# Loading the activation tiles of a banded-attention and MoE layer in pairs of two

## What is computed

```python
x = _layernorm(x + attn(x, w_q, b_q, w_k, b_k, w_v, b_v, w_o, b_o))
x = _layernorm(x + ffn(x, gate_w, gate_b, w1, b1, w2, b2))
# attn: q, k, v = x @ w + b; scores of each token with its 7 neighbours, softmax, @ v, @ w_o + b_o
# ffn:
logits = xf @ gate_w + gate_b
top_w, top_i = top_k(logits, 2)
comb = zeros(n, 8).at[arange(n)[:, None], top_i].add(softmax(top_w))
for ei in range(8):
    h = relu(xf @ w1[ei] + b1[ei])      # w1[ei]: 1024 x 4096
    y = h @ w2[ei] + b2[ei]             # w2[ei]: 4096 x 1024
    out = out + comb[:, ei:ei + 1] * y
```

## Time and profile before

| what | us |
|---|---|
| median of 2 runs | 4987.21 |
| the two runs | 4957.83 and 5016.59 |
| the profiled execution | 4956.09 |
| its span on the slowest core, from first to last instruction | 4953.2 |
| spans of the 8 cores | 4941.5 to 4953.2 |
| start to the first q matmul, half 0 | 77.65 |
| start to the first q matmul, half 1 | 2534.65 |

### The profile page before, as it was taken

How to read it: one execution, slowest core, us unless ns; L and a number is a source line. 1 busy time by engine, 2 the same in 40 slices (tenths; PEclk the granted TensorE clock), 3 DMA queues, 4 the chain that set the end, 5 groups by cost and what they waited for, 6 DMA issues and landing times. The chain is left out here.

```text
span 4953.2 us, 53689 instructions; the slowest of 8 cores (4941.5 to 4953.2 us)
## 1 busy us (share of the span) xinstructions
PE 4303.1 (87%) x19624; PEld 1913.9 (39%) x19624; DVE 1155.8 (23%) x3024; ACT 1091.2 (22%) x2172; POOL 148.7 (3%) x192
## 2 busy tenths in 40 slices
PE   4645589999999999999975554999999999999998
PEld 2222234444444444444432222344444444444443
DVE  0344411122211222111213444022111222112223
ACT  2222222211122111221242222211222111221113
POOL 0000000000000000000000000000000000000000
PEclk9656579999999999999986665899999999999999
DMA  5100034444454444444630000454444544544443
GB/s 86 19 13 9 5 56 80 68 79 75 69 84 69 76 78 68 79 75 72 104 76 17 13 9 6 66 82 69 76 78 68 82 72 71 83 69 77 77 68 85
DMA packets 149771, 310.94 MB, mean 63 GB/s; under 512 B 3641, under 2 KB 4025, under 8 KB 149453
## 3 DMA queue, kind: packets, MB, share of 16 engines
q0 software_dynamic: 144096, 289.49, 36.4%
q1 hardware_dynamic: 5422, 18.03, 1.1%
HBM read 588.60 MB, written 8.39 MB: 121 GB/s over the span
## 5 line engine op out<-in xcount | busy, mean ns | idle before, releaser
L999 PE MATMUL m_pY<-m_w2b,m_hg 128*128 128x512 bf16 x8192 | 1778.8, 379 | 74.1 <-ACT m_hg L976 72.7
L959 PE MATMUL m_pH<-s_xt,m_w1b 128*128 128x512 bf16 x8192 | 1782.2, 380 | 0.0
L1014 DVE SCALAR_TENSOR_TENSOR m_acc<-m_pY,s_comb,m_acc 128x512 f32<-128x512 f32 x1024 | 721.7, 747 | 2955.6 <-PE m_pY L999 2955.6
L976 ACT ACTIVATE m_hg<-m_pH,s_b1pc 128x512 bf16<-128x512 f32 x1024 | 705.9, 689 | 2859.4 <-PE m_pH L959 2859.4
L999 PEld LDWEIGHTS m_pY<-m_w2b,m_hg 128*128 128x128 bf16 x8192 | 796.6, 98 | 1056.3 <-issue 105.4
L959 PEld LDWEIGHTS m_pH<-s_xt,m_w1b 128*128 128x128 bf16 x8192 | 802.4, 98 | 971.8 <-issue 7.9
L510 PE MATMUL h_pj<-h_v_tm,h_attnT 128*128 128x64 bf16 x256 | 54.4, 212 | 261.8 <-DVE h_attnT L503 261.8
L465 ACT ACTIVATE h_a_bf<-h_smx,h_nmx 128x134 bf16<-128x134 f32 x256 | 104.4, 408 | 360.4 <-DVE h_nmx L455 340.7
L510 PEld LDWEIGHTS h_pj<-h_v_tm,h_attnT 128*128 128x128 bf16 x256 | 26.8, 105 | 302.2 <-issue 302.2
L286 PE MATMUL h_pj<-h_xt_ext,s_wbuf 128*128 128x512 bf16 (+1 forms) x640 | 118.7, 344 | 27.2 <-PEq L57 27.2
L447 DVE SCALAR_TENSOR_TENSOR h_smx<-h_pj,s_consts,s_masks 128x134 f32<-128x134 f32 x176 | 61.3, 349 | 295.1 <-PE h_pj L437 294.5
(11 more groups left out here) (95 smaller groups left out, 1213.8 us busy)
## 6 DMA issues: line engine op xcount, KB each, us to landing
m_w1b<-w POOLq DMA_DIRECT2D x64, 2048.0 KB, 16.0
m_w2b<-w POOLq DMA_DIRECT2D x64, 2048.0 KB, 15.9
h_x_own<-xh SPq DMA_DIRECT2D x16, 512.0 KB, 3.4
out<-s_ostg SPq DMA_DIRECT2D x16, 512.0 KB, 2.7
s_xb<-xh POOLq DMA_DIRECT2D x16, 256.0 KB, 3.8
s_wbuf<-wq POOLq DMA_DIRECT2D x2, 2048.0 KB, 25.0
s_wbuf<-wk POOLq DMA_DIRECT2D x2, 2048.0 KB, 36.3
s_wbuf<-wv POOLq DMA_DIRECT2D x2, 2048.0 KB, 15.9
```

Source lines behind the costliest of these rows:

```text
L959: e.matmul(pH[jj % 2][:, 0:512], w1b[0][:, ic * GCOLS + j * 128: ic * GCOLS + j * 128 + 128], xt1[:, ic * HALF_T + ts * 512: ic * HALF_T + ...
L976: e.activation(hg[:, j * HALF_T + ts * 512: j * HALF_T + ts * 512 + 512], pH[jj % 2][:, 0:512], AF.Relu, bias=b1pc[:, e_i * 32 + g_i * 8 + ...
L999: e.matmul(pY[t % 2][fs][:, 0:512], hg[:, j * HALF_T + t * 128: j * HALF_T + t * 128 + 128], w2b[0][:, j * GCOLS + fs * 512: j * GCOLS + f ...
L1014: e.scalar_tensor_tensor(acc[:, t * D + fs * 512: t * D + fs * 512 + 512], pY[t % 2][fs][:, 0:512], comb[:, t * 8 + e_i: t * 8 + e_i + 1], ...
```

## The change

The loads of tiles 2 to 7 of a half are made in pairs. After the transposes of tiles 1, 3 and 5 one DMA, `emit_xld_pair`, brings tiles t + 1 and t + 2, 256 consecutive rows, into both slots of `xb`. It waits for the last transpose of both of the tiles that were there. Both tiles then count on the semaphore `sXB0`. Tile 8 is loaded as before, after the transposes of tile 6. Nothing is issued any more after the transposes of tiles 0, 2 and 4. The rest is unchanged.

```diff
+                def emit_xld_pair(t):
+                    src = xh_d.ap()[B + t * 128: B + t * 128 + 256, :]
+                    src = src.rearrange("(a p) n -> p a n", p=128)
+                    dst = xb[:, 0:2 * D].rearrange("p (a n) -> p a n", a=2)
+                    ev = p.op("pool",
+                              lambda e, src=src, dst=dst:
+                              e.dma_start(dst, src),
+                              waits=[xtr_ev[(t - 2, 7)], xtr_ev[(t - 1, 7)]],
+                              inc="sXB0", k=16)
+                    xld[t] = ev
+                    xld[t + 1] = ev
...
-                    if t + 2 < 9:
-                        emit_xld(t + 2)
+                    if t in (1, 3, 5):
+                        emit_xld_pair(t + 1)
+                    elif t == 6:
+                        emit_xld(8)
```

## The result

The kernel with pairs takes 0.55% longer: the ratio to before is 1.0055, with a 95% interval of 1.0040 to 1.0069. Of 4950 us this is 27 us (20 to 34). Of all executions the medians are 4992.98 us (43 of them, from 4977.99) and 4969.46 us (42, from 4950.13); disturbed executions of several hundred us are among both, and the ratio leaves them out. The profiled execution of the kernel after took 4986.8 us, that of before 4956.1 us.

The account below looks back on a forecast made before the run. TensorE, busy 87% of the span, was taken to bound the kernel, with A1 made of exposed waits. Delays of 14.4 us (half 0) and 14.2 us (half 1), together 28.6 us on 4956.1 us, gave 4985 us; range 4968 to 5045.

Parts of the forecast that it names:

- L: Time in block A1 from a pair's issue to its first tile's first transpose: 5.61 us in half 0, 6.23 in half 1.
- the rounds: Two tiles' turn in A1, costing 6.35 + L us: 12.0 us in half 0 and 12.6 us in half 1.
- The delay: Later start of tile 6 in A1, reaching the end 1:1: 14.4 us in half 0, 14.2 us in half 1.
- The sum: Delays of both halves' A1 together: 28.6 us, put on the profiled execution's 4956.1 us.
- Half 1's singles: Single tile loads in A1 of half 1, issue to first transpose: mean 4.49 us, against 3.87 in half 0.
- The further 256 KB: A pair's additional bytes over a single load in A1, claimed to add 1.74 us to L.
- the slope: Load time from 256 KB (3.8 us) to 2048 KB (16.0 us): 1.74 us per further 256 KB, used for L.
- The cheap pair: Rival in A1: L within 0.5 us of a single's, mostly latency; 19.5 us slower, 4976 us; chance 0.22.
- The dear pair: Rival in A1: the pair's two blocks handled one behind the other; 43 us slower, 4999 us; chance 0.12.
- the much slower one: Rival in A1: pair spread over few DMA engines, L 30 us; 173 us slower, 5129 us; chance 0.03.
- Half 0 hiding its delay: Rival in half 0's A1: wk's landing does not move, only half 1 pays; 14.2 us, 4970 us; chance 0.02.
- Faster: Rival in A1: fewer loads pay the fixed part fewer times, saving 12 us, 4944 us; chance 0.01.

Follow-up runs that it names:

- e1: Kernel after, but pairs in half 0 only, half 1 loading its tiles singly; ratio to before 1.0040, median core 4960.7 us.
- e2: Kernel after, but pairs in half 1 only, half 0 loading its tiles singly; ratio to before 1.0041, median core 4960.4 us.
- e6: Kernel before with tile 8's transposes and copies in half 1 done seven times, loads unchanged; ratio to before 1.0019, median core 4961.4 us.
- e9: Kernel before with wk's load in half 0 issued in the block after A1; ratio to before 0.9975, median core 4934.5 us.
- the control: Kernel before, unchanged, run once more; ratio to before 0.9999, median core 4947.2 us.
- e4: Kernel before, but each single load of tiles 2 to 8 issued only after the previous tile's last transpose; ratio to before 1.0113, median core 4996.7 us.
- e3: Kernel after with two 256 KB loads in place of each pair, issued at the same moment; ratio to before 1.0049, median core 4966.4 us.
- e7: Kernel after, but pairs and tile 8 loaded into v's buffer, issued at A1's start without a wait; ratio to before 0.9956, median core 4926.1 us.

## Why the prediction was right and where it was wrong

**What was right.** The mechanism held step by step. The odd tiles wait for no load, the even ones for all of L; TensorE's releaser is the load each time; the rounds are 12.07 and 11.68 us where 12.0 was said, and 11.75 and 11.95 us in half 1 where 12.6 was said. A pair's transposes take 6.35 us in two rounds as read from before, 6.6 us in two others. The delay goes to the end 1:1 in both halves (e1, e2, e6), and wk's landing carries it in half 0 (e9). The sum, 28.6 us, stands against 26.4 us in A1, 27.6 us on the median core and 27 us by the ratio. The measured median of 4992.98 us lies in the range of 4968 to 5045.

**The step that failed: the base that the sum was put on.** The sum of +28.6 us was put on the profiled execution of 4956.1 us and gave 4985 us. But the kernel before had been given as a median of 4987.2 us, of two executions that were 59 us apart. Set beside that median, 4985 us says "2 us faster", the opposite of the text's own sum. The text saw that the profiled execution stood at the lower of the two, and used it for the width of the range only. What the runs showed in its place: the kernel after is slower by 27 us (1.0040 to 1.0069), from 4969.5 to 4993.0 us by the medians of all executions. Of the 42 executions of before 21 lie between 4950 and 4966 us and 19 at 5016.6 us or more, so that a median of two could fall anywhere between, and neither 4987.2 nor 4956.1 us was its median. The profiled base did serve for the profiled execution, for which 4984.7 us was forecast and 4986.8 us measured. Core 7's loss of 15 us adds only 4.5 us to that, since core 6 stood at 4979.6 us; that the two nearly cancel against a sum some 2 us too high in A1 is luck. A forecast in us that is read against a median should have carried the sign: the difference first, and the base with it. In the same way "within 2%" was right, while the interval of 1.0040 to 1.0069 excludes no change, and the forecast of a kernel slower by 0.6% should have been stated as plainly.

**Terms that were mis-sized.** Half 1's singles, 4.67, 4.68 and 4.11 us on the page's core, were taken as a price that half 1 has in itself. That was one core's scatter in the main: the singles of tiles 2, 4 and 6 of before, over the eight cores, take 4.11 us in half 0 (3.65 to 4.81) and 4.32 us in half 1 (3.72 to 5.24), and the control has 4.17 us in both. Alone, in e4, they take 3.97 and 4.13 us, so a neighbour in flight costs 0.2 us or less on average. The pair is 5.65 us in half 1 where I had 6.23 us. The further 256 KB were put at 1.74 us by the slope to the 2048 KB load; they cost 1.5 to 1.6 us. The far end of that slope was high: the 16.0 us of the earlier trace rows are 14.7 us on the page of after, and wk alone in e9 takes 14.5 us, which gives (14.5 - 3.97) / 7 = 1.50 us. In half 0, 5.61 us stands against 5.53 us. POOL's issue of a pair takes 0.71 us instead of 0.53 us, which the text had at no difference. It is part of L.

**The rivals.** The cheap pair (19.5 us) comes near the time of two singles on the same schedule: e3 has 17.8 us. It fell because one landing stands for both tiles. The dear pair (43 us) and the much slower one (173 us) fell, with L at 5.5 to 5.7 us. Half 0 hiding its delay fell in e1. Faster fell: L is far above 0.8 us. The page's formula for a load from GpSimd (the Trainium skill, DMA: Bandwidth & Descriptors, "Anatomy of one DMA"), by which a further 256 KB cost 0.6 us, is not borne out here, where they cost 1.5 us. Counted by the 512 KB of floats that are read for them, that formula gives an estimate of 1.2 us, which is nearer and still too low. Its rule to issue early and wait late (same page, "Rules for kernel authors") is: the lost overlap is 17.8 of the 26.4 us, and e7, which issues the same pairs early, is 22 us faster than before.

## What to carry to other kernels

Joining two loads into one saved nothing here, since their issue waited for TensorE before and after. It cost the first consumer the second one's bytes, and with two buffers it also took both at once, so that the load could no longer fly over the work. If loads are to be joined, have as many buffers as are needed to issue them early; space that only a later stage uses can serve. Look also at what a block's end waits for: a load that only the next block needs, issued before that end, held TensorE for 13 us here.

## What the runs showed of the hardware

One core of eight can run the projections of its attention at a granted clock of 1.2 GHz where the others of the same execution have 2.4 GHz again, and then it is 11 to 16 us late. When it is the slowest core it sets the time of the whole program. In the profiled executions it is seen with pairs in half 1 (after), with pairs in half 0 alone (e1), with single loads (e3) and with the loads issued ahead (e7), so it is not tied to the pairs' delay. With such cores a measured ratio can be off by more than 0.1% when there are only a few executions: e1's is 1.0040, where its median core is longer by 0.25%. The spans of all cores tell more than the time of the slowest.
